# An xLSTM and MLP block on one core: VectorE transposes the first heads, their projection moves behind the products of tile 14

## The reference

```
q, k, v, o = xn Wq.T, xn Wk.T, xn Wv.T, xn Wog.T      (8 heads; 32 per head in q and k, 64 in v)
i, f       = softcap15(xn Wig.T + big), softcap15(xn Wfg.T + bfg)
per head, over time: m' = max(logsig(f) + m, i);  F = exp(logsig(f) + m - m');  I = exp(i - m')
                     C = F C + I k v^T;  n = F n + I k;  h = C.q / (max(|n.q|, exp(-m')) + eps)
h     = headwise normalised h * gamma
out   = x + (sigmoid(o) * h) Wout.T + (silu(xn Wgate.T) * (xn Wup.T)) Wdown.T      (2048 hidden)
```

## Time and profile before

| what | value |
|---|---|
| median of 3 runs | 3109.54 us (3109.21 to 3110.54) |
| the profiled execution's own time | 3110.59 us |
| its span | 3108.9 us |
| granted TensorE clock, mean | 0.998 |
| busy: TensorE, VectorE, ScalarE, GpSimd | 98%, 75%, 36%, 25% of the span |
| one block, from its gates products to the next block's | 94.50 us |

### The profile page before, as it was taken

The page is one execution under the profiler, slowest core; times in us unless marked ns, Lnnn a source line. Parts: engine busy times, 40 slices in busy tenths (PEclk is TensorE's granted clock), DMA queues, the critical chain, the costliest instruction groups (busy, mean ns, idle before and its releaser), DMA issues.

```text
span 3108.9 us, 62468 instructions
## 1 busy us (share of the span) xinstructions
PE 3047.3 (98%) x22090; PEld 2194.9 (71%) x22090; DVE 2347.1 (75%) x5913; ACT 1113.4 (36%) x2160; POOL 781.7 (25%) x1121
## 2 busy tenths in 40 slices
PE   4999999999999999999999999999999999999999
PEld 2677777777777777777777777777777777777776
DVE  7877777777777777777777777777777777777777
ACT  6333333333323333333333333333233333333332
POOL 4222222222222222222222222222222222222222
PEclk9999999999999999999999999999999999999999
DMA  5000000000000000000000000000000000000000
GB/s 224 8 14 13 13 7 7 13 13 13 13 0 13 13 13 13 7 7 13 13 13 13 7 7 13 13 13 13 0 13 13 13 13 7 7 13 13 13 13 7
DMA packets 20334, 51.09 MB, mean 16 GB/s; under 512 B 1506, under 2 KB 1634, under 8 KB 18274
## 3 DMA queue, kind: packets, MB, share of 16 engines
q1 hardware_dynamic: 20322, 50.95, 4.4%
HBM read 34.16 MB, written 16.78 MB: 16 GB/s over the span
## 4 chain that ended last, share of the span: by engine, by line
issue 73%; POOL 22%; PE 2%; DVE 1%; POOLq 1%; ACT 1%; DMA 0%; SPq 0%; DVEq 0%; ACTq 0%
POOL arena L555 9%; POOL pair_r L545 4%; POOL small L574 3%; POOL arena L565 2%; POOL begun L562 1%; POOL small L462 1%; DVE amax L757 1%; PE work L1154 0%; POOLq L554 0%; DMA arena<-w_v_dram 0%; POOL small L464 0%; POOL small L467 0%; POOL small L460 0%; PE work L1119 0%; ACT weights L611 0%
## 5 line engine op out<-in xcount | busy, mean ns | idle before, releaser
L1117 PE MATMUL work<-xt,weights 128*128 128x256 f16 x4608 | 1256.0, 273 | 0.0
L1119 PE MATMUL work<-xt,weights 128*128 128x256 f16 x4608 | 1256.0, 273 | 0.0
L1118 PE MATMUL work<-xt,weights 128*128 128x256 f16 x4608 | 1255.9, 273 | 0.0
L555 POOL TENSOR_TENSOR arena<-arena 128x256 f16<-128x256 f32 x512 | 359.5, 702 | 1628.2 <-ACT arena L689 1628.2
L689 ACT ACTIVATE arena<-arena 128x256 f16<-128x256 f32 x512 | 213.3, 417 | 1057.8 <-DVE arena L983 1057.8
L1117 PEld LDWEIGHTS work<-xt,weights 128*128 128x128 f16 x4608 | 478.5, 104 | 69.2
L1118 PEld LDWEIGHTS work<-xt,weights 128*128 128x128 f16 x4608 | 450.9, 98 | 69.7
L1119 PEld LDWEIGHTS work<-xt,weights 128*128 128x128 f16 x4608 | 450.8, 98 | 52.3
L1117 PE MATMUL acc<-weights,arena 128*128 128x512 f16 x1024 | 388.1, 379 | 0.5 <-POOL arena L555 0.5
L1118 PE MATMUL acc<-weights,arena 128*128 128x512 f16 x1024 | 388.1, 379 | 0.0
L1119 PE MATMUL acc<-weights,arena 128*128 128x512 f16 x1024 | 388.1, 379 | 0.0
(11 more groups left out here) (212 smaller groups left out, 4150.7 us busy)
## 6 DMA issues: line engine op xcount, KB each, us to landing
arena<-x_dram SPq DMA_DIRECT2D x33, 512.0 KB, 3.4
out_dram<-arena SPq DMA_DIRECT2D x32, 512.0 KB, 2.8
weights<-w_g_dram SPq DMA_DIRECT2D x4, 1024.0 KB, 13.2
weights<-w_u_dram SPq DMA_DIRECT2D x4, 1024.0 KB, 20.4
arena<-w_d_dram SPq DMA_DIRECT2D x4, 1024.0 KB, 27.2
arena<-w_qk_dram SPq DMA_DIRECT2D x1, 1024.0 KB, 6.3
arena<-w_v_dram SPq DMA_DIRECT2D x1, 1024.0 KB, 8.3
weights<-w_o_dram SPq DMA_DIRECT2D x1, 1024.0 KB, 25.4
```

Source lines behind the costliest of these rows:

```text
L555: g.tensor_tensor(hh[:, j % HB, 1, :], tt[:, j % 2, :], hh[:, j % HB, 0, :], ALU.subtract).then_inc(h_ready, 1)
L1117: t.matmul(dst, w[0], a[0], start=first, stop=False, skip_group_check=True)
L1118: t.matmul(dst, w[0], a[1], start=False, stop=False, skip_group_check=True)
L1119: return t.matmul(dst, w[1], a[0], start=False, stop=last, skip_group_check=True)
```

## The change

- The transposes of the first chunk's heads, `hoT0`, leave TensorE. VectorE makes them in four steps `hturn00` to `hturn03` of four 32x128 transpositions each, from `hof` to an SBUF region `hot`: one step in tile 11, two in tile 13, one in tile 14. Then `hoT0` is only ScalarE's copy and VectorE's subtraction, both from SBUF, now in tile 14 and not 11.
- The second heads get a buffer of their own (`hof2`), as does each chunk's split (`hoh` is doubled).
- In tile 14, `heads1` stands first, then `hturn03` and `hoT0`.
- `project(0)` moves from tile 13 to behind `down(14)`, and with it VectorE's `add_mlstm(0)`, to the block's end.
- `att0` and `att1` use work banks 0 and 1 instead of 1 and 2, and `hoT0` uses none.
- In tiles 4, 6 and 8, VectorE's `es` step, which waits for the mask, stands last.

```diff
-         "ffn6", "st0", ... "ffn11", "hoT0", "ffn12", "st3", "o1",
-         "ffn13", "att0", "ffn14", "ffn15", "hoT1", "att1"])
+         "ffn6", "st0", ... "ffn11", "ffn12", "st3", "o1",
+         "ffn13", "ffn14", "ffn15", "hoT1", "att0", "att1"])
+BANK["att0"], BANK["att1"] = 0, 1
-AFTER[11] = ["hoT0", "turn12", "turn13"]
+AFTER[11] = ["turn12", "turn13", "hturn00"]
 AFTER[12] = ["pv3", "o1", "center1"]
-AFTER[13] = ["att0", "scale1"]
-AFTER[14] = ["heads1"]
+AFTER[13] = ["scale1", "hturn01", "hturn02"]
+AFTER[14] = ["heads1", "hturn03", "hoT0"]
 AFTER[15] = ["hoT1", "xT0", "xT1"]
+DVE_AFTER[4] = ["wbc", "kturn0", "kturn1", "es0"]
+DVE_AFTER[6] = ["pv0", "turn01", "es1"]
+DVE_AFTER[8] = ["pv1", "es2", "center0"]
 DVE_AFTER[10] = ["heads0", "pv2", "es3"]
...
-        sq = at["hof"].rearrange("p (h e) -> p h e", h=NH)
+        sq = at["hof2"].rearrange("p (h e) -> p h e", h=NH)
+        hot = arena[:, starts["bc"]:starts["bc"] + D]
+        ho = at["hoh"].bitcast(F16).rearrange("p (c a k t) -> p c a k t", c=NCH, a=2, k=KC)
...
 ScalarE, hoT:
-                            wait_full(act, i, step)
+                            if k == 0:
+                                act.wait_ge(heads_turned, START + (i + 1) * TURNS)
+                            else:
+                                wait_full(act, i, step)
...
 VectorE:
+                        elif step.startswith("hturn"):
+                            dve.wait_ge(ho_ready, START + i * NCH + 1)
+                            turn(hot, hof, k_, heads_turned)
-                        elif step == "att0":
-                            add_mlstm(i, 0)
                 for c in range(NCH):
-                    if c == 1:
-                        add_mlstm(i, 1)
+                    add_mlstm(i, c)
...
 TensorE:
                 def project(c):
-                    wait_drained(pe, i, f"hoT{c}")
+                    if c == 0:
+                        pe.wait_ge(ho_split, i + 1)
+                    else:
+                        wait_drained(pe, i, "hoT1")
...
-                        elif step == "att0":
-                            project(0)
                 down(NJ - 2)
+                wait_bank(pe, i, "att0")
+                project(0)
                 down(NJ - 1)
                 wait_bank(pe, i, "att1")
                 project(1)
```

More of the change, by code:

```diff
@@ L55 @@
 USES = (["gates", "q", "k", "v0", "v1", "ffn0", "ffn1", "ffn2", "ffn3", "wT", "ffn4", "wbc", "ffn5", "o0",
-         "ffn6", "st0", "ffn7", "ffn8", "st1", "ffn9", "ffn10", "st2", "ffn11", "hoT0", "ffn12", "st3", "o1",
-         "ffn13", "att0", "ffn14", "ffn15", "hoT1", "att1"])
+         "ffn6", "st0", "ffn7", "ffn8", "st1", "ffn9", "ffn10", "st2", "ffn11", "ffn12", "st3", "o1",
+         "ffn13", "ffn14", "ffn15", "hoT1", "att0", "att1"])
 NUSE = len(USES)
 BANK = {name: n % 3 for n, name in enumerate(USES)}
+BANK["att0"], BANK["att1"] = 0, 1
 def bank_no(name):
@@ L234, in mlstm_mlp_kernel @@
                  ("mm", 256), ("upd", GW), ("num", NH * VW),
-                 ("hof", 512), ("hoh", 512), ("kp", 512), ("tt", 512), ("hh", 768), ("res", 1024),
+                 ("hof", 512), ("hof2", 512), ("hoh", 1024), ("kp", 512), ("tt", 512), ("hh", 768), ("res", 1024),
                  ("wtok", NCH * 72), ("qq", 1024), ("kk", 1024),
@@ L290, in mlstm_mlp_kernel @@
         kp = at["kp"].bitcast(F16).rearrange("p (a g t) -> p a g t", a=2, g=NG)
-        ho = at["hoh"].bitcast(F16).rearrange("p (a k t) -> p a k t", a=2, k=KC)
+        hot = arena[:, starts["bc"]:starts["bc"] + D]
+        ho = at["hoh"].bitcast(F16).rearrange("p (c a k t) -> p c a k t", c=NCH, a=2, k=KC)
         tt = at["tt"].rearrange("p (b t) -> p b t", b=2)
@@ L341, in mlstm_mlp_kernel @@
         xn_turned = sem("xn_turned")
+        heads_turned = sem("heads_turned")
+        ho_split = sem("ho_split")
         kt_ready = sem("kt_ready")
@@ L531, in _ @@
             for n, started in enumerate((*work_free, out_stored, res_done, exp_done, p_ready, num_ready, ho_ready,
-                                         state_ready, xn_turned)):
+                                         state_ready, xn_turned, heads_turned)):
                 g.memset(begun[0:1, n:n + 1], 0.0).then_inc(started, START)
@@ L717, in _ @@
                         elif step.startswith("hoT"):
-                            wait_full(act, i, step)
-                            s.activation(ho[:, 0, :, :], bank(step)[:, :].rearrange("p (k t) -> p k t", k=KC),
-                                         ACT.Copy).then_inc(ho_hi, 1)
+                            if k == 0:
+                                act.wait_ge(heads_turned, START + (i + 1) * TURNS)
+                            else:
+                                wait_full(act, i, step)
+                            s.activation(ho[:, k, 0, :, :], (hot if k == 0 else bank(step)[:, :]).rearrange(
+                                "p (k t) -> p k t", k=KC), ACT.Copy).then_inc(ho_hi, 1)
                         elif step.startswith("xn"):
@@ L817, in means, with turn @@
                     d.bn_aggr(mean_var[:, c, :], bn6[:, c, :]).then_inc(stats_ready, 1)
-            def turn(dst, src, q):
+            def turn(dst, src, q, done):
                 tokens = slice(q * 32, (q + 1) * 32)
@@ L824, in turn @@
                     d.transpose(dst.rearrange("p (k t) -> p k t", k=KC)[r * 32:(r + 1) * 32, :, tokens],
-                                features).then_inc(xn_turned, 1)
+                                features).then_inc(done, 1)
             def x_low(i, c, src):
@@ L1077, in _ @@
                             wait_drained(dve, i, f"o{k_}")
-                            d.scalar_tensor_tensor(out=hof.rearrange("p (h e) -> p h e", h=NH),
+                            d.scalar_tensor_tensor(out=(hof, at["hof2"])[k_].rearrange("p (h e) -> p h e", h=NH),
                                                    in0=to.rearrange("p (h e) -> p h e", h=NH), scalar=1.0,
@@ L1083, in _ @@
                             dve.wait_ge(ho_hi, i * NCH + k_ + 1)
-                            d.tensor_tensor(ho[:, 1, :, :], bank(step)[:, :].rearrange("p (k t) -> p k t", k=KC),
-                                            ho[:, 0, :, :], ALU.subtract).then_inc(free_of(step), 1)
+                            ins = d.tensor_tensor(ho[:, k_, 1, :, :],
+                                                  (hot if k_ == 0 else bank(step)[:, :]).rearrange(
+                                                      "p (k t) -> p k t", k=KC),
+                                                  ho[:, k_, 0, :, :], ALU.subtract)
+                            ins.then_inc(ho_split if k_ == 0 else free_of(step), 1)
                         elif step.startswith("xT"):
@@ L1090, in _ @@
                             dve.wait_ge(xn_ready, NCH * (i + 1) + c + 1)
-                            turn(xnt[c], xn[c], k_)
+                            turn(xnt[c], xn[c], k_, xn_turned)
+                        elif step.startswith("hturn"):
+                            dve.wait_ge(ho_ready, START + i * NCH + 1)
+                            turn(hot, hof, k_, heads_turned)
                         elif step.startswith("kturn"):
@@ L1192, in project @@
                 def project(c):
-                    wait_drained(pe, i, f"hoT{c}")
+                    if c == 0:
+                        pe.wait_ge(ho_split, i + 1)
+                    else:
+                        wait_drained(pe, i, "hoT1")
                     for n in range(KC):
-                        mm_ = three(bank(f"att{c}")[:, :], (ho[:, 0, n, :], ho[:, 1, n, :]),
+                        mm_ = three(bank(f"att{c}")[:, :], (ho[:, c, 0, n, :], ho[:, c, 1, n, :]),
                                     (w_out[:, 0, n, :], w_out[:, 1, n, :]), n == 0, n == KC - 1)
@@ L1289, in _ @@
                                      stop=True).then_inc(work_full, 1)
-                        elif step.startswith("hoT"):
+                        elif step == "hoT1":
                             pe.wait_ge(ho_ready, START + i * NCH + k + 1)
                             for n in range(KC):
-                                tr = t.transpose(bank(step)[:, n * P:(n + 1) * P], hof[:, n * P:(n + 1) * P],
+                                tr = t.transpose(bank(step)[:, n * P:(n + 1) * P], at["hof2"][:, n * P:(n + 1) * P],
                                                  ident[:, :])
                             tr.then_inc(work_full, 1)
-                        elif step == "att0":
-                            project(0)
                 down(NJ - 2)
+                wait_bank(pe, i, "att0")
+                project(0)
                 down(NJ - 1)
```

## The result

| | before | changed |
|---|---|---|
| median of the runs | 3109.38 us (3108.57 to 3110.54, 4 runs) | 3138.45 us (3137.99 to 3138.71, 4 runs) |
| span of the profiled execution | 3108.9 us | 3136.3 us |
| one block, gates products to gates products | 94.50 us | 95.40 us |
| mean granted TensorE clock | 0.998 | 0.998 |

The changed kernel is slower: the ratio is 1.0093, with a 95% interval of 1.0077 to 1.0109. 32 blocks at 0.90 us more make 28.8 us, and the medians differ by 29.07. The loop therefore holds the difference. The two profiled executions lie 27.4 us apart: the first gates products start at 74.62 us before and at 73.79 changed, and over the eleven traces of this case that start varies from 73.01 to 75.84, so a us or two outside the loop says nothing about the change.

What follows compares the result with a forecast made beforehand. TensorE, busy 94.25 of a block's 94.50 us, was taken as the bound. Terms -0.88, +1.58 and +0.22 give +0.92 us a block, +29.4 over 32 blocks: 3139 us after a 1.05 us correction, range 3108 to 3147.

Steps and rivals of the forecast that it cites:

- Part 1: Tile 11: hoT0's four transposes and the wait for VectorE's heads leave TensorE, -0.88 us a block.
- Part 2: Tiles 13 to 15: TensorE waits 0.65 us at hoT1 and 0.93 at project(0) for VectorE, +1.58 us a block.
- the chain: Steps from ScalarE's copy of the last head sums in tile 13 to the split first heads project(0) needs, 13.87 us.
- L1064 at tile 9's price: Small VectorE product in tile 13 takes 0.59 us beside GpSimd's L555, not 0.17; otherwise the wait is 1.16, not 1.58.
- Part 3: Block's end: q must wait for VectorE's read of att1 in the second work bank, +0.22 us a block.
- Part 4: Tiles 4, 6, 8: masks put last overlap up to 5.9 us a block of VectorE time, nothing for TensorE.
- the cover: Tile 13 starts with VectorE waiting for ScalarE, which hides tile 11's 12 transpositions, 4.0 us.
- The sum: Whole block: -0.88 + 1.58 + 0.22 = +0.92 us, +29.4 over 32 blocks, 3139 us, slower by 0.9%.
- Rival A: VectorE is in time: the chain starts from VectorE's own lag, masks bring it forward, 3088 us; chance 0.10.
- zero: Start of the chain: ScalarE's copy of the last head sums at 1573.00, after a 1.80 us wait for TensorE.
- Rival C: The clock falls: new idle time brings a half-clock stretch costing 1.65 us a block, about 3192 us; chance 0.02.
- Rival B: Both edges soft: L1064 not held, transpositions overlap, heads1 quicker, wait 0.66 paid by part 1, 3109.5 us; chance 0.10.

Runs made afterwards that it cites:

- experiment 6: The kernel before, with only the es steps of tiles 4, 6 and 8 of VectorE put in the new order: 3095.95 us, ratio 0.9952.
- Experiment 4: The changed kernel with hturn01 in tile 12 ahead of center1 instead of in tile 13: 3096.14 us, ratio 0.9955.
- experiment 5: The kernel before, with project(0) and its addition moved behind the products of tile 14, hoT0 still on TensorE: 3110.72 us, ratio 1.0000.
- experiment 1: The changed kernel with hturn01 ahead of scale1 in tile 13 of VectorE instead of behind it: 3129.58 us, ratio 1.0062.
- experiment 2: The changed kernel with att1 on work bank 2 instead of 1: 3134.15 us, ratio 1.0076.
- experiment 3: The changed kernel with the es steps in tiles 4, 6 and 8 of VectorE back in their old order: 3151.03 us, ratio 1.0134.

## Why the prediction was right, and where it was not

The forecast was 3139 us and slower; 3138.45 was measured. By its own steps:

- **Part 1, -0.88.** Right in size: no wait and no transposes stand in tile 11 of the changed kernel. But half of it, the 0.41 us wait at hoT0, was not hoT0's: experiment 6 shows that the mask order alone removes it. The change holds two cures for that one wait.
- **Part 2, +1.58.** Right in mechanism, and 0.06 too small in size. The late starts are 0.54 and 1.04 us against 0.65 and 0.93. The first is shorter since TensorE started 0.05 us behind VectorE and not 0.14. The second is set by the chain, which is 13.94 us long against 13.87; 0.05 of that is ScalarE's copy from SBUF, whose price the prediction took from a copy out of a work bank. Experiment 4 takes 1.34 us of transpositions out of it and gets 1.33 back; experiment 5 shows that without them the move costs nothing.
- **L1064 at tile 9's price.** Right: 0.59, and experiment 1 moves it back to 0.17. That price decided between 1.58 and 1.16. The Trainium skill's page "SBUF — State Buffer" has it that a VectorE instruction with two SBUF inputs contends with a GpSimd instruction that reads SBUF ("Who interferes with whom"). The trace agrees: 0.59 us with GpSimd's subtraction under way, 0.17 without.
- **Part 3, +0.22.** Mis-sized: 0.14 by both the timeline and experiment 2. The step that failed is "1592.72 + 0.14": the 0.14 was taken from hoT0's start, and q starts 0.06 us after VectorE's end.
- **Part 4, masks "nothing for TensorE".** Wrong in what it left out. The forecast did not suffer, since part 1 had already booked the wait at hoT0 as gone; but with the masks in their old order the changed kernel takes 3151 us, not 3138. As a statement of what the edit is worth, "nothing" missed 0.39 us a block with the rest of the change (experiment 3) and 0.45 without it (experiment 6). The prediction looked only at who uses the masks, not at who uses what VectorE does after them. And it named center1 as what would be late if the cover went; it was the bank of ffn12.
- **The sum, +0.92.** Measured +0.90: 0.54 + 1.04 at the late starts, 0.06 between them for the slower transposes at hoT1, 0.14 at q, less 0.88. The slower transposes are no loss of their own: TensorE waits for the end of VectorE's chain just behind them, and without them that wait would be 0.06 longer. So part 2 came to 1.64 and not 1.58, part 3 to 0.14 and not 0.22, and the two misses nearly cancel. That 3139 fell within 1 us of 3138.45 is in so far luck; the terms were good to 0.08 us a block, some 3 us.
- **Rival A** said that the chain might start from VectorE's own lag. It does not: ScalarE's copy at zero waits 2.86 us for TensorE, and with VectorE 1.6 us later (experiment 3) hoT1 and project(0) are as late as in the changed kernel, to 0.01 us. **Rival C**, the clock: the block holds 1.00. **Rival B** had L1064 at 0.17 us and a wait of 0.66; the trace has 0.59 and 1.58, and experiment 1 shows that the 0.59 was real time in the chain.

## What to carry to other kernels

Where one engine is full, moving its work to an engine with room pays only if the work lands where that engine waits. With twelve transpositions in tiles 13 and 14 the kernel is 0.9% slower than before. With six of them in tile 12, where VectorE waited, and att1 back on bank 2, it is 0.95% faster; about half of that gain is the mask order's, which both kernels have. Look for the receiving engine's waits just ahead of the start of the chain that sets the deadline. And when pricing a wait on a helper engine, ask not only who uses its result, but who uses everything queued behind it: the waits for masks that nobody needed soon held up heads and banks that TensorE needed at once.

## What the runs showed of the hardware

- How soon TensorE starts after the event that it waited for was not one number: 0.14 us at hoT0 before, 0.05 at hoT1 (1594.22 + 1.04 = 1595.26 to 1595.31), 0.15 at project(0) (1597.30 + 0.69 = 1597.99 to 1598.14), 0.06 at q. Why they differ was not tried.
- Four transposes behind a wait took 0.47 to 0.50 us to the next product, and 0.44 without a wait.
- A VectorE product of two 128x8 tensors took 0.59 us when GpSimd's subtraction was under way and 0.17 when not, and the order of two steps chose between them (experiment 1). At a seam into a transposition, VectorE started 0.11 us later than into a reduction.
- att1 on bank 2 also shortened VectorE's wait for the mask, from 43.2 to 23.8 us in total, and lengthened its wait at center1 from 66.0 to 86.8, though TensorE came only 0.14 us earlier. The rows show where VectorE gained: at the state update L1043 of `pv0` in tile 6, next to GpSimd's product L552. Changed kernel, then att1 on bank 2:

```profile
1551.30 2.29 DVE L1043 SCALAR_TENSOR_TENSOR arena<-arena,small 128x264 f32<-128x264 f32 x1
1551.42 1.89 POOL L552 TENSOR_TENSOR pair_r<-arena,diag 40x1024 f16<-40x1024 f16 x1
...
1550.79 0.52 DVE L1043 SCALAR_TENSOR_TENSOR arena<-arena,small 128x264 f32<-128x264 f32 x1
1551.00 2.06 POOL L552 TENSOR_TENSOR pair_r<-arena,diag 40x1024 f16<-40x1024 f16 x1
```

  With its start 0.12 us ahead of GpSimd's, VectorE's operation ended 0.28 us behind it, after 2.29 us; with 0.21 us it took 0.52. Over the run, L1043 is busy for 121.3 us in the one kernel and 76.2 in the other. Neither wait holds TensorE in that kernel. No experiment moved this pair by itself, so that GpSimd's product is the cause is read from the rows and not tested.
